# Second graph layer's projection: features copied out of the product's bank by ScalarE, the maximum taken from the copy

## The reference, cut to what matters

```
h  = (x @ W).reshape(N, H, D)
el = einsum('nhd,hd->nh', h, al);  er = einsum('nhd,hd->nh', h, ar)
e  = leaky_relu(el[src] + er[dst]);  ex = exp(e - segment_max(e, dst)[dst])
out = segment_sum(ex / s[dst] * h[src], dst) + b;  return elu(out)
```

## Time and profile before

| | us |
|---|---|
| median of 3 runs (lowest, highest) | 2088.42 (2086.89, 2089.89) |
| the profiled execution | 2085.56 |
| its span, first to last instruction | 2083.8 |
| busy over the span: PE / DVE / ACT | 1690.7 (81%) / 1561.6 (75%) / 1345.5 (65%) |
| line 739, 60 copies of scores in three projections | 160 to 191 ns each |
| lines 740 and 741, 60 each | 410 to 416 ns each |
| mean granted TensorE clock | 0.943 of full speed |

### The profile page before, as it was taken

One profiled execution on the slowest core, in us unless ns is written; L12 is line 12 of the kernel. 1 busy time (PEld: TensorE's weight loads), 2 busy tenths in 40 slices (PEclk: granted clock), 3 DMA queues, 4 the chain that ended last, 5 costly groups with the idle time before them and its releaser, 6 DMA issues. The chain is left out here.

```text
span 2083.8 us, 62466 instructions
## 1 busy us (share of the span) xinstructions
PE 1690.7 (81%) x21608; PEld 1337.5 (64%) x21608; DVE 1561.6 (75%) x3518; ACT 1345.5 (65%) x2207; POOL 279.2 (13%) x446
## 2 busy tenths in 40 slices
PE   3988873899989739998992799998989985688883
PEld 1222222888989528898891577775548973688883
DVE  6999988899999889999997522222333257899996
ACT  0257546999999569999994622221113365899986
POOL 2555510566600000000000000000000000000000
PEclk9999997999999969999996999999999997799997
DMA  2000000001100000100101200000010010000002
GB/s 74 17 2 2 2 1 27 28 28 41 40 29 28 1 30 28 41 32 35 40 16 55 94 2 0 0 0 8 0 36 24 20 59 14 14 21 22 21 22 101
DMA packets 34806, 54.83 MB, mean 26 GB/s; under 512 B 10708, under 2 KB 26256, under 8 KB 34448
## 3 DMA queue, kind: packets, MB, share of 16 engines
q1 hardware_dynamic: 30992, 51.59, 7.5%
q0 software_dynamic: 3584, 0.06, 0.1%
HBM read 43.14 MB, written 8.49 MB: 25 GB/s over the span
## 5 line engine op out<-in xcount | busy, mean ns | idle before, releaser
L1106 ACT ACTIVATE Rm<-rows,cB 128x1280 bf16<-128x1280 f32 (+3 forms) x816 | 847.2, 1132 | 32.5 <-DVE Mn L1141 19.3
L1243 PE MATMUL ps<-R,M 128*128 128x132 f16 (+1 forms) x8640 | 684.5, 221 | 117.3 <-DVE Mn L1141 62.8
L1243 PEld LDWEIGHTS ps<-R,M 128*128 128x128 f16 x8640 | 545.6, 97 | 141.4 <-DVE M L1151 51.7
L1151 DVE TENSOR_TENSOR M<-Rm,C 128x1280 f16<-128x1280 bf16 (+3 forms) x816 | 528.4, 674 | 37.2 <-ACT Rm L1106 27.0
L1236 PE MATMUL ps<-HB,C 128*128 128x66 f16 x6400 | 304.1, 194 | 60.5 <-DVEq L1132 60.5
L1236 PEld LDWEIGHTS ps<-HB,C 128*128 128x128 f16 x6400 | 258.9, 98 | 60.7 <-DVEq L1132 60.7
L642 PE MATMUL acc<-ohc,ohl 128*128 128x500 f16 x806 | 216.2, 380 | 42.3 <-DVE ohl L596 33.4
L1154 DVE SCALAR_TENSOR_TENSOR M<-rows,cN,C 128x1280 f16<-128x1280 f32 (+1 forms) x144 | 217.2, 1509 | 0.0
L593 DVE TENSOR_SCALAR ohc<-cells,near 128x1000 f16<-128x1000 f16 x403 | 196.5, 488 | 17.1 <-PE acc L642 10.5
L642 PEld LDWEIGHTS acc<-ohc,ohl 128*128 128x128 f16 x806 | 52.9, 97 | 198.1 <-DVE ohl L596 161.9
L431 POOL DMA_INDIRECT wd<-wv,wi x112 | 135.2, 1207 | 151.3 <-issue 106.9
(11 more groups left out here) (296 smaller groups left out, 2257.5 us busy)
## 6 DMA issues: line engine op xcount, KB each, us to landing
rows<-rowd SPq DMA_DIRECT2D x32, 640.0 KB, 3.9
rows<-rowd SPq DMA_DIRECT2D x16, 320.0 KB, 3.4
xd<-R SPq DMA_DIRECT2D x4, 640.0 KB, 2.9
xr<-xd SPq DMA_DIRECT2D x20, 128.0 KB, 2.0
xd<-HB SPq DMA_DIRECT2D x1, 2560.0 KB
xr<-xd SPq DMA_DIRECT2D x5, 512.0 KB, 7.0
R<-in_x SPq DMA_DIRECT2D x1, 2432.0 KB
xr<-in_x SPq DMA_DIRECT2D x19, 128.0 KB, 2.0
```

The source lines that it names most:

```text
L1106: a.activation(Rm[:, s % SG, 0:wide(p)], rows[:, p % 2, 0:wide(p)], ACT.Relu, bias=cB[:, ds(h + s * nh, 1)]).then_inc(s_R, 1)
L1151: v.tensor_tensor(M[:, u, 0:wide(p)], Rm[:, u, 0:wide(p)], Cs, ALU.min).then_inc(s_M if s in ONE else s_cut, 1)
L1243: m = pe.matmul(region(p % 2, r), lhsT, rhs, start=split and opens and r % 3 == 0, stop=True, skip_group_check=True)
```

## The change

Only the branch `norm=False` changes its order. `result` stays for the other two projections. In this one VectorE copies the scores, now as the first step of a trip; ScalarE copies the features (`features`, a fourth activation per tile, after `turned`); VectorE takes the maximum in the next trip from the copy in HV (`largest`). A new semaphore s_hv counts the copies. A product waits for the copy of tile t-2 in place of its three results.

```diff
@@ VectorE
+                    def scores(t):
+                        v.wait_ge(s_M, t + 1)
+                        v.tensor_copy(scores_of[:, :, :, t],
+                                      psH[t % 2][:, D:W2].rearrange("p (j h) -> p j h", j=2)).then_inc(s_out, 1)
+
+                    def largest(t):
+                        v.wait_ge(s_hv, t + 1)
+                        v.tensor_reduce(hmax[:, t:t + 1], HV[:, t, :, 0:dh], AX.XY, ALU.max, apply_absolute_value=True)
...
-                        for i in range(NT + 4):
+                        for i in range(NT + 5):
+                            if 0 <= i - 4 < NT:
+                                scores(i - 4)
                             if i < NT:
                                 biased(i)
                             if 0 <= i - 2 < NT:
                                 unit(i - 2)
-                            if i >= 4:
-                                result(i - 4)
+                            if i >= 5:
+                                largest(i - 5)
@@ ScalarE
+                    def features(t):
+                        a.wait_ge(s_out, t + 1)
+                        a.activation(HV[:, t, :, 0:dh], psH[t % 2][:, 0:D].rearrange("p (h c) -> p h c", c=dh),
+                                     ACT.Copy).then_inc(s_hv, 1)
...
-                        for i in range(NT + 3):
+                        for i in range(NT + 4):
                             if i < NT:
                                 negative(i)
                             if 0 <= i - 1 < NT:
                                 power(i - 1)
-                            if i >= 3:
+                            if 0 <= i - 3 < NT:
                                 turned(i - 3)
+                            if i >= 4:
+                                features(i - 4)
@@ TensorE
-                        if t >= 2:
+                        if t >= 2 and norm:
                             pe.wait_ge(s_out, (t - 1) * 3)
+                        elif t >= 2:
+                            pe.wait_ge(s_hv, t - 1)
```

More of the change, by code:

```diff
@@ L695, in attention @@
                 psH = [ph.ps(f"psH{u}", [P, W2]) for u in range(2)]
-                s_z, s_r, s_e, s_bn, s_mv, s_sd, s_rs, s_y, s_T, s_xT, s_M, s_out = (
-                    ph.sem(n) for n in ("z", "r", "e", "bn", "mv", "sd", "rs", "y", "T", "xT", "M", "out"))
+                s_z, s_r, s_e, s_bn, s_mv, s_sd, s_rs, s_y, s_T, s_xT, s_M, s_out, s_hv = (
+                    ph.sem(n) for n in ("z", "r", "e", "bn", "mv", "sd", "rs", "y", "T", "xT", "M", "out", "hv"))
                 block = ph.enter_context(nc.Block())
```

## The result

| | before | changed |
|---|---|---|
| median, us (4 runs each) | 2088.44 | 2126.58 |
| lowest to highest | 2086.89 to 2089.89 | 2123.99 to 2127.38 |
| ratio, 95% interval | | 1.0182, 1.017 to 1.0194 |

The forecast was 2107.3 with a range of 2103.5 to 2113.0: the direction was right, the size half of the measured 38.1 us, and the time lies outside the range.

The account below looks back on a forecast made before the run. A chain of waits, two tiles in 3.47 us, was taken as the bound, becoming 2.81 per tile. Late fill 3.13, half clock 0.3, 15 loops of 42.15 and tail 1.5 gave +18.9 on 2088.42: 2107.3 us, range 2103.5 to 2113.

Parts of the forecast that it names:

- What bounds the kernel: In this projection no engine is full; a chain of waits through VectorE, ScalarE and TensorE advances two tiles in 3.47 us.
- The wait moved to the head: Scores' copy first in VectorE's trip holds back the next z: the loop closes after one tile, z following 0.09 us behind.
- The sum 2.81: Steady loop per tile: 0.45+0.32+0.31+0.42+1.22+0.09 = 2.81 us, taken over 15 loops as 42.15 us.
- The features' copy at nothing: ScalarE's copy after `turned`, 0.36 to 0.42 us, fits its idle time: no cost in the steady part.
- the maximum at nothing: VectorE's maximum from memory one trip later is hidden; the 0.33 us per tile freed in its list gains nothing.
- the estimate of 65 ns less: VectorE's reduction from SBUF instead of PSUM: 1.3 us over 20 tiles if VectorE were the limit, here hidden.
- The fill: At the projection's start z(4) stands behind scores(0), which wait for the first product: it starts 3.13 us late.
- I add 0.3 for its part at half clock: Second product in the fill runs partly at half clock, the rise taken at about 707.6: 0.3 us, between 0 and 2.0.
- the drain: From the last z to the last maximum: 8.58 us against 7.08 before, a tail of 1.5 us more.
- Rival A: TensorE's clock falls in the loop's gaps: product 2.18, loop 3.81 us, 2125 us (2116 if half the time); 8 in 100.
- B: Faster: products ready when VectorE asks, pace TensorE's 1.51 us per tile, 4.5 us less, 2083.9; 5 in 100.
- C: Half the cost: the loop keeps two tiles, bounded by TensorE's 1.51, plus late fill and tail: 2088.5 us; 3 in 100.

Follow-up runs that it names:

- scores last: The changed kernel with VectorE's scores copy moved to the end of its trip, features still copied by ScalarE: 2085.0 us, ratio 0.9985.
- six pieces of extra work: The changed kernel with two unread identity transposes on TensorE behind each of the first six products only: 2122.82 us, ratio 1.0175.
- the extra work: The changed kernel with two identity transposes on TensorE, into an unread bank, behind each product: 2110.02 us, ratio 1.0111.
- two orders changed: The changed kernel with ScalarE's `turned` ahead of `negative` and TensorE's `product(i-1)` ahead of `turn(i)`, scores still at the head: 2094.73 us, ratio 1.003.

## Why the prediction was half right

- **What bounds the kernel: right.** The loop of two tiles in 3.47 us was the pace; two of the loop's steps taken out of it (scores last) gave 2.81 for two tiles, as the sum has it.
- **The wait moved to the head: right.** One tile per loop, shown with it alone (2125.77) and by taking it alone away (2085.0). z followed the scores by 0.09, so the value taken for that spacing held. The sum 2.81 was met exactly, but only where the clock was full.
- **The features' copy at nothing, the maximum at nothing: right.** The copy took 0.37, ScalarE had time. A maximum read from memory took 0.41, as from the bank; the estimate of 65 ns less, drawn from the Trainium skill, "VectorE: DVE Perf Modes", section on the TRN2 errata, does not show.
- **The fill: right in length** (3.13), **wrong in the clock.** "I add 0.3 for its part at half clock; between 0 and 2.0" is the step that failed. It took the time of the rise, 707.6, from a kernel whose TensorE had worked without a pause from its first turn, and put it into one that pauses after the first product. This term, put at 0.3 us, came out at 14.9 in the 15 loops (57.08 against 42.15), and the drain, which the sum took at full clock, at 3.7 more than its 8.58: 18.3 us over the forecast in all. The bound of two slow products was a guess about when the rise would come, and the case that it does not come was left to a rival of 8 in 100.
- **Rival A was the case,** down to its numbers: loop 3.81 against 3.80 measured, time 2125 against 2126.6. In one point it differed: A has the clock fall in the gaps, and here it never rose; the fall is seen only in the run with six pieces of extra work. The argument against it was weak where it counted. The earlier trace rows show two stretches of 3.4 us at full level with 51 and 57% busy; they say that a short thin stretch is survived, not that many loops are. The run with the six pieces shows just that: three thin loops at full level, then the fall. The Trainium skill's sentence in "TensorE: Matmul & The Clock Gate", section on a second failure mode, on a clock that swings where TensorE idles briefly between groups pointed the right way; in the changed kernel it did not swing but stayed low.
- **Rivals B and C were rightly small.** B's fixed point, that no product can be ready at the head of the trip, held in every run with the wait at the head; but what that wait costs hangs on the others' orders, as the run with two of them changed shows. The 1.51 us per tile that both took as TensorE's limit was none: 1.405 and 1.16 were measured.

What stays open is what decides when the clock rises: with the extra work it came about 23 us after TensorE's first turn in one run and about 15 us after it in the other, under the same 3.49 of 4.00 us busy, and with two orders changed 5.5 us after it, under 3.28 and 3.30. That the loop's gaps cost the clock is shown, by filling them and by leaving them empty again; how long or how frequent a gap has to be is not.

## What to carry to other kernels

Before moving a wait to another place in an engine's list, walk the loop through all engines' lists and count how many tiles it spans: the same sum of steps is paid once per that many. A wait at the head of a trip is harmless only if nothing it waits for is queued, on any engine, behind something this trip has yet to issue. And price every loop that leaves TensorE gaps twice, at the full and at the half clock: a change that thins its work out can lose the clock too, and here that doubled the cost.

## What the runs showed of the hardware that was not expected

- Clock: with TensorE working without a pause from 702.2 it was at full level by about 707.6 (kernel before), and with pauses of 0.47 us from 702.99 by about 708.5 (two orders changed). With a pause of about 0.5 us in each 3.8 (3.49 of 4.00 busy) it stayed at 0.50 for some 15 us in one run and 23 us in the other, and then rose. In the changed kernel, with pauses of 0.93 us and 2.87 to 3.46 of 4.00 busy, it did not rise from 703 to 771. The run with two orders changed had 3.05 of 4.00 busy and stayed at 1.00, so the recorded busy time alone does not tell the level.
- A full clock was kept through three loops with TensorE busy 1.62 of 2.81 us and lost after them (one profiled execution, six pieces of extra work).
- The busy time summed from the profile is no floor for TensorE: 1.51 us per tile by that sum, 1.405 and 1.16 measured, as the recorded lengths of neighbouring matmuls overlap.
